# The inverse of the attention row sums moved from VectorE to POOL in an attention and fast-feedforward kernel

## What is computed

```python
Q1, Q2 = split(Q); K1, K2 = split(K)          # 16 heads, each with two maps of width 16
attn = softmax(Q1 K1^T * s) - lamb * softmax(Q2 K2^T * s)
out  = layernorm((attn @ V) @ Wo) * gamma + beta
x    = x + out + ffn(xn)                      # ffn: three tree-routed 16-leaf MLPs give q, k, v
                                              # of a second softmax attention
```

## Time and profile before

| what | value |
|---|---|
| median of three runs | 4075.53 us (4073.76 to 4076.94) |
| the profiled execution's own time | 4072.35 us |
| its span | 4070.5 us |
| PE busy | 3755.0 us (92%) |
| DVE busy | 3159.8 us (78%) |
| ACT busy | 2786.5 us (68%) |
| POOL busy | 1103.3 us (27%) |
| mean granted clock of TensorE | 0.965 |

### The profile page before, as it was taken

The page is one execution under the profiler, slowest core; times in us unless marked ns, Lnnn a source line. Parts: engine busy times, 40 slices in busy tenths (PEclk is TensorE's granted clock), DMA queues, the critical chain, the costliest instruction groups (busy, mean ns, idle before and its releaser), DMA issues. The chain is left out here.

```text
span 4070.5 us, 63429 instructions
## 1 busy us (share of the span) xinstructions
PE 3755.0 (92%) x23714; PEld 1470.7 (36%) x23714; DVE 3159.8 (78%) x5580; ACT 2786.5 (68%) x3267; POOL 1103.3 (27%) x1520
## 2 busy tenths in 40 slices
PE   6998599999999999999999999999999859899999
PEld 4773122222222222222222222222222236578888
DVE  5457599989999998999999899999999413344444
ACT  3441388888888887888888788888888936522221
POOL 3211013204113212310411231032123157662420
PEclk9997699999999999999999999999999979999999
DMA  5546601111011111111111111111101069832320
GB/s 181 188 162 234 221 29 43 38 49 50 27 48 40 38 48 36 42 38 50 32 37 51 32 38 40 48 32 45 43 22 43 22 235 333 254 115 64 100 83 21
DMA packets 224694, 330.88 MB, mean 81 GB/s; under 512 B 29298, under 2 KB 165237, under 8 KB 219781
## 3 DMA queue, kind: packets, MB, share of 16 engines
q1 hardware_dynamic: 173988, 244.61, 18.5%
q0 software_dynamic: 18432, 50.36, 3.8%
q10 hardware_dynamic: 31968, 31.85, 2.4%
HBM read 169.34 MB, written 156.34 MB: 80 GB/s over the span
## 5 line engine op out<-in xcount | busy, mean ns | idle before, releaser
L1616 DVE TENSOR_REDUCE arena<-psum 128x1 f32<-128x512 f32 x4096 | 2558.5, 681 | 218.3 <-PE psum L1282 200.9
L1470 ACT ACTIVATE arena<-psum,exp_scale 128x1024 f32<-128x1024 f32 x2048 | 2157.7, 1110 | 298.8 <-PE psum L1320 288.9
L1282 PE MATMUL psum<-arena 48*128 48x512 f16 x4096 | 1314.1, 394 | 157.9 <-ACT arena L1430 55.9
L1336 PE MATMUL psum<-arena 128*32 128x512 f32 x8200 | 1107.1, 612 | 1.2 <-ACT arena L1470 0.6
L1282 PEld LDWEIGHTS psum<-arena 48*128 48x128 f16 x4096 | 317.1, 93 | 1808.4 <-DVE arena L1616 1487.0
L1320 PE MATMUL psum<-arena 50*128 50x512 f16 x4096 | 901.7, 384 | 15.9 <-ACT arena L1470 9.2
L1510 POOL TENSOR_TENSOR arena<-arena 128x16 f32<-128x16 f32 x129 | 28.4, 220 | 2123.7 <-DVE arena L1626 2123.7
L991 ACT ACTIVATE mix_arena<-psum,mix_arena 128x1024 f32<-128x1024 f32 x64 | 71.3, 1114 | 329.6 <-DVE mix_arena L1011 329.6
L1336 PEld LDWEIGHTS psum<-arena 128*32 128x32 f32 x8200 | 162.2, 108 | 258.0 <-issue 256.5
L1320 PEld LDWEIGHTS psum<-arena 50*128 50x128 f16 x4096 | 214.0, 95 | 94.1 <-ACT arena L1470 79.4
L894 POOL DMA_INDIRECT mix_arena<-scratch_sorted_y,mix_arena x192 | 181.7, 946 | 235.6 <-PE psum L946 169.1
(11 more groups left out here) (168 smaller groups left out, 3315.4 us busy)
## 6 DMA issues: line engine op xcount, KB each, us to landing
arena<-scratch_split SPq DMA_DIRECT2D x762, 64.0 KB
scratch_split<-route_arena SPq DMA_DIRECT2D x64, 512.0 KB, 2.8
scratch_sorted_x<-arena ACTq DMA_DIRECT2D x60, 512.0 KB, 7.4
leaf_arena<-scratch_sorted_x SPq DMA_DIRECT2D x60, 512.0 KB, 5.8
scratch_sorted_y<-leaf_arena SPq DMA_DIRECT2D x60, 512.0 KB, 4.1
leaf_arena<-in_leafw SPq DMA_DIRECT2D x3, 5128.0 KB, 18.9
arena<-in_x SPq DMA_DIRECT2D x18, 512.0 KB, 4.7
scratch_sum<-arena SPq DMA_DIRECT2D x18, 512.0 KB, 3.0
```

The costliest lines, as they stand in the source:

```text
L1282: nc.tensor.matmul(aux_bank[bank], ring[at, slot, 0, m, qt * P:(qt + 1) * P], ring[at, slot, 1, m, c * CH:(c + 1) * CH], start=True, stop=True
L1336: last = nc.tensor.matmul(value_bank[32 * j:32 * j + 32, :], vaug[:, batch % 2, kt, 2 * pair + j % 2, :], prob[:, step % 2, j, :], start=k ...
L1470: nc.scalar.activation(prob[:, step % 2, 2 * h:2 * h + 2, :], score[:, 2 * h:2 * h + 2, :], ACT.Exp, scale=exp_scale[:, s % 2, s // 2:s // ...
L1616: nc.vector.tensor_reduce(halfmax[:, odd, 2 * m + h, qt, c:c + 1], aux_bank[bank], AX.X, ALU.max).then_inc(bank_used[bank], 1)
```

## The change

`invert` goes from VectorE, with its two waits for ACT's copy in each set and the one in the epilogue, and with the semaphore `inverse_ready`. `join_maps` on POOL waits for ACT's copy itself, and makes the inverse: the power -1 of the 16 sums into `linv`, then one Newton step in three small instructions (`lres = linv * total`, `lres = 2 - lres`, `linv = linv * lres`), each behind a wait for the one before, on the same semaphore `ochain` (six counts per join in place of two). Two small tiles are added, and one memset of 16 elements on VectorE at the stage's start. The three instructions of the join that were there stay.

```diff
     linv = ar.take(NCH, 4, PARTS)
+    lres, minus_one = ar.take(4, PARTS), ar.take(4, PARTS)
...
             def join_maps(n, s, c):

-                pool.wait_ge(inverse_ready, n + 1)
+                total, done = osum[:, c, :, :, HD], n * 6
+                nc.gpsimd.tensor_tensor(linv[:, c], total, minus_one, ALU.pow).then_inc(ochain, 1)
+                pool.wait_ge(ochain, done + 1)
+                nc.gpsimd.tensor_tensor(lres, linv[:, c], total, ALU.mult).then_inc(ochain, 1)
+                pool.wait_ge(ochain, done + 2)
+                nc.gpsimd.tensor_scalar(lres, lres, -1.0, 2.0, ALU.mult, ALU.add).then_inc(ochain, 1)
+                pool.wait_ge(ochain, done + 3)
+                nc.gpsimd.tensor_tensor(linv[:, c], linv[:, c], lres, ALU.mult).then_inc(ochain, 1)
+                pool.wait_ge(ochain, done + 4)
                 nc.gpsimd.tensor_tensor(linv[:, c], linv[:, c], sign, ALU.mult).then_inc(ochain, 1)
-                pool.wait_ge(ochain, n * 2 + 1)
+                pool.wait_ge(ochain, done + 5)
...
+                    wait_read(pool, place(i, s, 5, "o", 1))
                     join_maps(2 * n, (s - 1) % PER_BATCH, 1)
...
+                    wait_read(pool, place(i, s, 11, "o", 0))
                     join_maps(2 * n + 1, s, 0)
...
+            wait_read(pool, START[BATCH] + EPILOGUE.index(("o", 1)))
             join_maps(BATCH * 2 * PER_BATCH, PER_BATCH - 1, 1)
...
+            nc.vector.memset(minus_one, -1.0)
...
-            def invert(c):
-
-                nc.vector.reciprocal(linv[:, c], osum[:, c, :, :, HD]).then_inc(inverse_ready, 1)
...
-                        if step == 7:
-                            wait_read(dve, place(i, s, 5, "o", 1))
-                            invert(1)
-                        if step == 13:
-                            wait_read(dve, place(i, s, 11, "o", 0))
-                            invert(0)
...
-            wait_read(dve, START[BATCH] + EPILOGUE.index(("o", 1)))
-            invert(1)
```

More of the change, by code:

```diff
@@ L1090, in attention_stage @@
     nmax_ready, mparts_ready, shift_in = sem("nmax_ready"), sem("mparts_ready"), sem("shift_in")
-    inverse_ready, oset_ready = sem("inverse_ready"), sem("oset_ready")
+    oset_ready = sem("oset_ready")
     zeros_ready, vaug_ready, sign_ready = (
@@ L1514, in join_maps @@
                                         ).then_inc(ochain, 1)
-                pool.wait_ge(ochain, n * 2 + 2)
+                pool.wait_ge(ochain, done + 6)
                 maps = omul.rearrange("p q (m h) d -> p q m h d", m=2)
```

## The result

The changed kernel takes 4056.97 us (median of five runs, 4049.76 to 4058.08), the kernel before 4074.76 us in the same comparison (4071.16 to 4076.94). The ratio is 0.9953 with a 95% interval from 0.9939 to 0.9968, so it is faster, by 17.8 us by the medians (0.4%; the interval reaches from 13 to 25 us). The profiled executions differ by 14.3 us (4072.35 and 4058.08; spans 4070.5 and 4056.2). The forecast was -13.1 us, 4062.4, in a range from 4055 to 4073.

What follows compares the result with a forecast made beforehand. The ordinary step was taken as set at 2.49 us by a loop through TensorE's order and a bank, not VectorE alone. Terms -7.4 - 6.1 + 0.4 = -13.1 us gave 4062.4 by the median (4059.3 profiled), range 4055 to 4073.

Steps and rivals of the forecast that it cites:

- rival (c): VectorE's queue: every removed instruction pays, 128 x 0.16 = 20.5 us less the hidden ones, time 4052; chance 0.04.
- Part 1: Reciprocal in step 7, the join step: 2.74 us becomes 2.58, gain 46 x 0.16 = 7.4 us.
- 17 hidden ones: Step 7 reciprocals expected to gain nothing: 16 sets s = 0 and 1 under output projections, one in the last batch.
- Part 2: Reciprocal in step 13: VectorE's spare time per step covers it, gain taken as 0, at most 7.4 us.
- Part 3: POOL's chain: each join 4.5 us longer, 580 us more of POOL's time, all beside other work, results not late.
- D: Time of POOL's power on 16 elements, taken as 3.5 us, with nearest bounds 1.05 and 4.2 us.
- Rival (a): Collision falls the wrong way: D below 2.65 us, VectorE meets line 1771; about 4062 to 4075, centre 4070; chance 0.22.
- Part 4: Set 1, step 14: earlier `finish` shortens VectorE's `tensor_scalar` collision with POOL, 0.76 us x 8 = 6.1 us gain.
- Part 5: Epilogue: nothing hides the longer join, loss 0.4 us (0 with a short power, 1.1 with 4.2).
- signs of being wrong: Included a wait of TensorE for POOL (lines 1290 or 1725) that wasn't there before.
- (b): Step 7: TensorE's loop takes back the 0.16 us, leaving -6.1 + 0.4, so 4070; chance 0.13.
- (d): Slower: POOL's power slows VectorE's maxima beside it, each 1% costing 4.4 us; 4089 at 6%; chance 0.06 together.

Runs made afterwards that it cites:

- no_newton: The changed kernel without its Newton step, three small POOL instructions less per join: 4064.11 us, ratio 0.9980 to the kernel before.
- power2: The changed kernel with POOL's power done twice in each join: 4064.78 us, ratio 0.9982 to the kernel before.
- power3: The changed kernel with POOL's power done three times in each join: 4064.01 us, ratio 0.9980 to the kernel before.

## Why the prediction was right

**What bounds the stage** held. The long step was the join step, and the spare time in the others took the reciprocal of step 13: those steps went from 2.490 to 2.487 us. The Trainium skill ("VectorE: DVE Perf Modes", section "The DRAIN you can't avoid") has the pipe emptied behind every VectorE instruction, by which I had all 128 pay in rival (c). It speaks of the engine's own queue: the trace shows a step shorter by 0.003 us for the half of them that stood in step 13.

**Part 1** had the right mechanism and place, and its size was off: 46 x 0.16 = 7.4 us was forecast, 46 x 0.10 = 4.6 measured. The step that failed took the distance from the reciprocal's start to the next instruction's for its price. The instructions behind it make up part of that, which the timeline of before would have shown in a narrower window. The 17 hidden ones were hidden. The spare time of an ordinary step is 0.10 us, not a few hundredths.

**Part 2**: 0 forecast, 0.003 us per step measured.

**Part 3**: D was 2.91 us, not 3.5. The row on 4 elements (1.02 to 1.05 us) and this one give 0.16 us per element and a fixed part of 0.4 us, twice a multiplication's 0.2. I had put all above a multiplication on the elements. (The line goes through two points only. Rival (a)'s remark that multiplications have almost no fixed part was wrong: they take 0.20 us on 4 elements and 0.22 on 16, so nearly all is fixed.) POOL's busy time came to 1567.9 us, not 1680, for the same reason. Nothing waits for POOL in the steps.

**Part 4** was right in its mechanism and in how it hangs on D: at D between 2.65 and 3.5 the gain was to grow towards 1.4 us each, and it was 1.38, 11.0 us over 8 batches where 6.1 was forecast for D = 3.5. What it left out is the clock behind the stall. The excess at step 14 fell by 17.3 us, 6.3 more than the instruction, and rose by 5.8 at steps 1 to 3, where no instruction changed (170 ns each). The clock's record fits both: at step 14 it stood at 0.5 for 3.4 us in four batches and for 6.8 in four before, and for 3.4 in six and not at all in two after; at steps 1 to 3 for 3.4 us in seven and not at all in one before, and for 3.4 in five and 6.8 in three after. These two nearly cancel in this execution. They need not in each: the five runs of the changed kernel are ordered by mean granted clock, 4049.76 us at 0.968, 4054.36 at 0.967, 4056.97 at 0.966, 4057.99 and 4058.08 at 0.965.

**Part 5**: 0.4 us forecast, nothing found. With 2.91 us for the power the same sum has POOL free at 3248.5, just before the variance is there. The time from ACT's last copy to `finish` was 5.61 us before and is 5.61 after:

```profile
3242.75 0.41 ACT L1437 ACTIVATE arena<-psum 128x272 f32<-128x272 f32 x1
...
3248.77 1.02 POOL L1756 TENSOR_TENSOR arena<-arena 128x4 f32<-128x4 f32 x1 [0.20 <-DVE arena L1749]
```

One of my signs of being wrong did come there: TensorE's last transposes now wait for POOL's longer join.

```profile
3248.72 1.94 PE L1726 MATMUL psum<-arena 128*128 128x128 f32 x8 [2.51 <-POOL arena L1527]
```

It costs nothing, as the second `finish` stands in POOL's queue behind the first: from ACT's last copy to POOL's last wide instruction it is 32.26 us before and 32.24 after.

So the sum, 7.4 + 6.1 - 0.4 = 13.1, was 4.6 + 11.0 = 15.6 in the parts it was made of: one term too large by 2.8 us and one too small by 4.9. That the sum came close is in part luck. The medians differ by 17.8 us, more than these parts; the rest isn't attributed, and the five times of the changed kernel alone spread over 8.3 us.

**Rivals.** (a), a collision the wrong way, didn't come, as D was over 2.65, by 0.26 us only; `no_newton` and `power2` produced such a collision. (b) fell: the join steps got shorter. (c) fell by step 13. (d), maxima slowed by a power beside them, fell: in the changed kernel's trace the maxima that lie wholly beside a power take 681 ns each (median of 375), as those beside no power do, and where VectorE doesn't wait they follow each other every 0.598 us; with three powers the steps sum to 3.2 us less than in the changed kernel.

## What to carry to other kernels

Price a removed instruction by the length of the step that holds it, not by its duration or its place in the queue. A long instruction of POOL and a short one of VectorE on SBUF can meet at one place per batch, and a few tenths of a microsecond of work on either side move that meeting; look for the one instruction of its kind that takes nine times its shortest time, and gate or remove it. Then look at the block that stalls TensorE: here spreading it out was worth 47 to 49 us, about three times the change.

## What the runs showed of the hardware

- POOL's power costs 2.91 us on 16 elements per partition and 1.02 to 1.05 on 4; a multiplication 0.22 and 0.20.
- A VectorE `tensor_scalar` on 4 elements took 0.17 us alone, and waited for the end of a wide POOL instruction in every run in which one lay over it (1.20, 1.56, 1.69 us). This agrees with the Trainium skill ("SBUF — State Buffer", section "Who interferes with whom"). The maxima, which read PSUM, didn't slow. Beside POOL's power on 16 elements the same `tensor_scalar` didn't wait, so that agreement doesn't reach to every instruction of POOL. From `power3`, in the epilogue:

```profile
3250.05 2.90 POOL L1516 TENSOR_TENSOR arena<-arena 128x16 f32<-128x16 f32 x1
...
3250.86 0.17 DVE L1754 TENSOR_SCALAR arena<-arena 128x4 f32<-128x4 f32 x1
```

- The maxima behind a reciprocal follow sooner: the two intervals behind it are 0.545 and 0.591 us in place of 0.598 (medians, kernel before). Behind the join of the maxima alone, short and on SBUF too, they are 0.598 (changed kernel).
- A stall of TensorE by the same block of statistics without a collision cost 1.82 to 1.86 us where the clock stayed, 2.85 to 3.17 where it stood at 0.5 for 3.4 us, and 4.35 to 4.44 where it did for 6.8 us (96 blocks in eight traces). What decides which of these a block gets stays open; no run here separated it.
